# Order of the late gates, the operand pieces and the first ring weights in an output projection

## The chip, the cores and the metric

The kernel runs on one core of a Trainium2 chip. The metric is device time in microseconds (us) of one execution, the median of the runs shown. Five engines work in parallel, each through its own list of instructions in program order, and wait for one another on semaphores: PE (TensorE matmul), DVE (VectorE), ACT (ScalarE), POOL (GpSimd) and SP (SyncE, which here issues DMA loads).

## What is computed

One decoder layer on x of 2 x 512 tokens and 1024 channels: `x = x + block(norm(x))`, then a quantized product with a context, then a feed-forward stage with reconstructed weights. The block, cut to the part that the change touches:

```python
    y = Y.reshape(B, L, D_INNER) * silu(z)
    return y @ w_out.T                       # output projection
...
    h = res + mamba2(h, ...)
    h2 = rmsnorm(h, ln2_w)
    mlp = silu(h2 @ gate_w.T) * (h2 @ up_w.T) @ down_w.T
    return res + mlp
```

## The kernel before

All products are made in a split form: an operand in float32 becomes a rounded "hi" part (made by ACT, a copy to the rounded type) and a "lo" remainder (made by DVE, value minus hi), and three matmuls (hi hi, hi lo, lo hi) stand for one.

**The output projection** is the loop `for n in range(BATCH * KT)` that PE, ACT and DVE each write out for themselves. It has 16 blocks; `h, o = divmod(n, KT)` gives the half of the tokens (h, 0 or 1; the batch element is `ORDER[h]`) and the output tile o (0 to 7). PE does 24 matmuls of 128x512 for a block (8 tiles of the inner dimension times 3, line 857) and counts `s_used` at its end. Weights are double buffered: at the head of turn n, once block n is done, ACT makes the hi part of the weights of block n+2 (`weights_hi`, line 1284) and DVE the lo part (`weights_lo`, line 1738), and PE waits for the latter (`s_ready`) before block n+2. DVE then adds the block's product to the residual (line 2358, `s_h`), ACT squares the sum (`rms_square`, line 1618) and DVE adds up the squares (`rms_add`, line 2336), for a normalization of each half whose sums PE multiplies out with two more matmuls (`rms_sums`, line 1003; for half 0 after block 9, for half 1 later).

**The gates.** What the projection reads is y times silu(z). For half 1 these are made within the blocks of half 0: in turn o, ACT computes silu of tile o (`z_silu`, line 1590) and DVE multiplies (`make_y`, line 2268); one turn later ACT makes the hi part (`y_hi`, line 1586) and DVE the lo part (`y_lo`, line 2273). The eighth tile's hi and lo come at the end of turn 7. Block 8 (half 1, o = 0) needs the tiles in order of k.

**The feed-forward stage** that follows (`plain`, line 1031 for PE) starts on half 0's normalized values. Its operands have names: b11 (channel tiles 0 to 3 of half 0) and b21 (tiles 4 to 7), each of four pieces kk; b12 and b22 are the same of half 1. A piece is made by DVE (`make`, line 1877: residual times a parameter times the root), split by ACT (`part_hi_of`, line 1414) and DVE (`part_lo_of`, line 1906). In the loop of the projection, after the root of half 0 in turn 10 (`rms_root` on ACT, lines 1621 to 1624, `rms_rsqrt` on DVE, lines 2341 to 2344), turn 11 makes all of b11 and turn 13 all of b21. Weights of that stage go through a ring of seven slots: ACT `weight_hi` (line 1361), DVE `weight_lo` through `prefill` (line 1834). The seven slots are filled first in turns 14 and 15 by ACT and at the end of turn 14 by DVE. PE's order after block 15 is two steps of `plain` (12 matmuls each), the two matmuls of `rms_sums(1)`, which wait for the last `rms_add` of half 1, and then the rest of the feed-forward stage.

The order of the work on each engine is thus the order in which these lines are written out; no scheduler moves anything.

Of the kernel before, what the change touches and what calls it, by code (L numbers as in the profile page):

```python
# [8 lines left out]
ALU = mybir.AluOpType  # L9
# [21 lines left out]

ORDER = (1, 0)
Y_AT = {5: (0, 1, 2), 6: (3, 4, 5), 7: (6, 7)}
CTX_TILES = BATCH * KT

PART_AT = (0, 32, 64)
# [151 lines left out]
def build(nc, x_t, ctx, w_mamba, w_dt, w_gu, w_dn, f_gu, f_dn, b_gu, b_dn, params, shapes_only,  # L188
# [127 lines left out]
    def scr_c(j):  # L316
        return scr_c0[:, j, :] if j < 4 else scr_c1[:, j - 4, :]
# [186 lines left out]
    def part_hi(m, name):  # L504
        if name == "b12":
            return THr[m][2]
        return THr[m][3 if name == "b22" and m == 1 else RIGHT.index(name)]
# [4 lines left out]
    def value_of(m, name):  # L512
        if name in ("b11", "t2"):
            return VA[m]
        return TLf[m][{"b21": 6, "t4": 6, "b22": 5, "b12": 4, "t3": 4, "t1": 3}[name]]
# [760 lines left out]
    def _(act):  # L1276
# [125 lines left out]
        def part_hi_of(m, name):  # L1402

            if name == "t2":

                act.wait_ge(s_pd, fw(m, 6, 1) + 1)
            elif name == "t1" and m == 1:
                act.wait_ge(s_pd, fw(m, 7, 1) + 1)
            elif name == "t4":

                act.wait_ge(s_tlo, n_lo(m, "t2", KH - 1))
            for kk in range(KH):
                act.wait_ge(s_tv, N_MAKE[m, name, kk])
                act.activation(part_hi(m, name)[:, kk, :], value_of(m, name)[:, kk, :], ACT.Copy,
                               scale=-1.0 if name == "t2" else 1.0).then_inc(s_thi, 1)

        def move_b22():
            act.wait_ge(s_x2a, 32 * KT)
# [165 lines left out]
        def y_hi(h, k):  # L1584
            act.wait_ge(s_a, h * KT + k + 1)
            act.activation(ah(ORDER[h], k), xbc[:, 4 + k, HALF[ORDER[h]]], ACT.Copy).then_inc(s_ah, 1)

        def z_silu(h, k):
            act.wait_ge(s_z, h * KT + k + 1)
            act.activation(z_tile(h, k), z_tile(h, k), ACT.Silu).then_inc(s_zs, 1)  # L1590
# [29 lines left out]
        def rms_root(h):  # L1620
            act.preload_act_table_set("natural_log_exp_and_others")
            act.wait_ge(s_rv, h + 1)
            own.then(act.activation(rms_t[:, h, :], bank(6 + h), ACT.Ln, bias=EPS, scale=1.0 / DM))
            act.activation(rms_scale[:, h, :], rms_t[:, h, :], ACT.Exp, scale=-0.5).then_inc(s_hroot, 1)

        for n in range(BATCH * KT):
            h, o = divmod(n, KT)
            if N_OUT + n + 2 < N_MLP:
                weights_hi(N_OUT + n + 2, n % 2)
            if h == 0:  # L1630
                z_silu(1, o)
                if o >= 1:
                    y_hi(1, o - 1)
            elif o == 2:
                rms_root(0)
            elif o == 3:
                part_hi_of(0, "b11")
            elif o == 5:
                part_hi_of(0, "b21")
            elif o == 6:  # L1640
                for w in range(4):
                    weight_hi(w)
            elif o == 7:
                for w in range(4, RING):
                    weight_hi(w)
            rms_square(h, o)
            if n == KT - 1:
                y_hi(1, KT - 1)
        rms_root(1)

        feed_forward(0)
# [80 lines left out]
    def _(dve):  # L1732
# [133 lines left out]

        def make(m, name):

            va = VA[m]
            for kk in range(KH):  # L1870
                dst = value_of(m, name)[:, kk, :]
                if name in ("b11", "b12", "b21", "b22"):
                    k = kk if name in ("b11", "b12") else KH + kk
                    col = 0 if name in ("b11", "b21") else 1
                    half = COL[m][col]
                    if m == 0:
                        ins = STT(dst, hres[:, k, half], par[:, PL2 + k:PL2 + k + 1], rms_scale[:, col, :], ALU.mult, ALU.mult)
                    else:
                        ins = TT(dst, xc[:, k, half], scr_c(5)[:, half], ALU.mult)
                elif name == "t1":  # L1880

                    dve.wait_ge(s_tv, N_MAKE[m, "b12", kk])
                    ins = TT(dst, va[:, kk, :], value_of(m, "b12")[:, kk, :], ALU.subtract)
                elif name == "t3":
                    dve.wait_ge(s_tv, N_MAKE[m, "t1", kk])
                    ins = TT(dst, value_of(m, "b22")[:, kk, :], value_of(m, "b12")[:, kk, :], ALU.subtract)
                elif name == "t2":
                    dve.wait_ge(s_tv, N_MAKE[m, "t3", kk])
                    ins = TT(dst, value_of(m, "t3")[:, kk, :], va[:, kk, :], ALU.add)
                else:  # L1890
                    dve.wait_ge(s_tv, N_MAKE[m, "t2", kk])
                    ins = TT(dst, va[:, kk, :], value_of(m, "b21")[:, kk, :], ALU.subtract)
                ins.then_inc(s_tv, 1)
                if name in ("b11", "b21", "b12") and kk >= 1:
                    part_lo_of(m, name, kk - 1)
            if name in ("b11", "b21", "b12"):
                part_lo_of(m, name, KH - 1)

        def part_lo_of(m, name, kk):
            dve.wait_ge(s_thi, n_hi(m, name, kk))  # L1900
            dst, hi = part_lo(m, name)[:, kk, :], part_hi(m, name)[:, kk, :].bitcast(F32)
            src = value_of(m, name)[:, kk, :]
            if name == "t2":
                STT(dst, src, -1.0, hi, ALU.mult, ALU.subtract).then_inc(s_tlo, 1)
            else:
                TT(dst, src, hi, ALU.subtract).then_inc(s_tlo, 1)
# [439 lines left out]
        for n in range(BATCH * KT):  # L2346
            h, o = divmod(n, KT)
            half = HALF[ORDER[h]]
            if N_OUT + n + 2 < N_MLP:
                weights_lo(N_OUT + n + 3, n % 2, n % 2)  # L2350
            if h == 0:
                make_y(1, o)
                if o >= 1:
                    y_lo(1, o - 1)
            if o == 0:
                dve.wait_ge(s_reload[h], 16)
            dve.wait_ge(s_used, N_OUT + n + 1)
            TT(hres[:, o, half], hres[:, o, half], bank(n % 4), ALU.add).then_inc(s_h, 1)
            if o >= 2:
                rms_add(h, o - 1)  # L2360
            if n == KT - 1:
                y_lo(1, KT - 1)
            elif n == KT:
                rms_add(0, KT - 1)
            elif n == KT + 2:
                rms_rsqrt(0)
            elif n == KT + 3:
                make(0, "b11")
            elif n == KT + 5:
                make(0, "b21")  # L2370
            elif n == KT + 6:
                prefill(0, range(RING))
        rms_add(1, KT - 1)
        rms_rsqrt(1)

# [175 lines left out]
```

## Time and profile before

| | |
|---|---|
| median of 3 runs | 2105.76 us (2105.51 to 2106.44) |
| the profiled execution: its own time | 2103.68 us |
| its span in the profile | 2101.5 us |
| PE busy | 2073.0 us, 99% of the span |
| DVE busy | 1678.2 us, 80% |
| ACT busy | 1054.8 us, 50% |
| granted TensorE clock over the span | 0.999 |

The profile gives busy time by engine, a chain of work that ended last, and groups of instructions; the trace behind it answers questions about a stretch: what an engine did in order of time with the idle time in front of each instruction and what ended it (the timeline), who waited for whom (the waits), and busy shares with the granted clock by stretch (the windows). Times in those views count from the start of the span.

### The profile page before, as it was taken

How to read it: one execution, taken by the hardware profiler on the slowest of the kernel's cores; microseconds unless marked ns; L12 is line 12 of the kernel's file. 1: busy time of each engine (PE TensorE's matmuls, PEld its weight loads, DVE VectorE, ACT ScalarE, POOL GpSimd, SP SyncE). 2: the span in 40 equal slices, each digit the busy share in tenths (PEclk: the TensorE clock that was granted, in tenths of full speed). 3: DMA queues.
4: the chain of work that ended last, by engine and by line, in shares of the span. 5: the costliest groups of instructions: out<-in, count | busy, mean ns of one | idle time of the engine just before them, and what ended most of it. 6: DMA issues, size and time to landing. Idle time of an engine off the chain costs nothing.

```text
span 2101.5 us, 26518 instructions
## 1 busy us (share of the span) xinstructions
PE 2073.0 (99%) x9230; PEld 1671.1 (80%) x9234; DVE 1678.2 (80%) x2526; ACT 1054.8 (50%) x1748; POOL 185.3 (9%) x296
## 2 busy tenths in 40 slices
PE   8999999999999999999999999999999999999999
PEld 5777778788888888888888855888888888888887
DVE  7878686797777888888879899977777776698885
ACT  5333244457777777774444366533333333444442
POOL 0001101101111112110000002010000100100000
PEclk9999999999999999999999999999999999999999
DMA  3151116639889999897440045554444443846101
GB/s 136 40 201 60 51 61 200 145 114 324 295 295 335 328 347 350 293 344 264 140 141 1 1 180 127 171 186 147 176 150 174 152 152 126 322 172 211 50 21 61
DMA packets 136434, 370.07 MB, mean 176 GB/s; under 512 B 16688, under 2 KB 27568, under 8 KB 132656
## 3 DMA queue, kind: packets, MB, share of 16 engines
q1 hardware_dynamic: 110640, 287.12, 39.7%
q0 software_dynamic: 25088, 80.23, 11.3%
q8 instruction: 74, 1.21, 0.2%
q10 hardware_dynamic: 576, 1.05, 0.1%
q14 instruction: 56, 0.46, 0.1%
HBM read 288.12 MB, written 84.41 MB: 177 GB/s over the span
## 4 chain that ended last, share of the span: by engine, by line
PE 86%; DVE 9%; ACT 3%; issue 1%; DMA 1%; ACTq 0%; SPq 0%; DVEq 0%
PE pair L1087 47%; PE pair L1135 24%; PE pair L857 7%; PE pair L1031 2%; DVE conv_out L2171 2%; PE pair L850 1%; PE pair L1097 1%; DVE weights_lo L1738 1%; PE pair L969 1%; PE pair L990 1%; DMA sign_in_ab<-sign_spill 1%; PE pair L996 0%; DVE centred L2382 0%; ACT scratch_c L1675 0%; PE pair L992 0%
## 5 line engine op out<-in xcount | busy, mean ns | idle before, releaser
L1087 PE MATMUL pair<-comb_hi,ring_hi 128*128 128x512 f32 x1456 | 566.5, 389 | 0.0
L1087 PE MATMUL pair<-comb_hi,ring_lo 128*128 128x512 f32 x1456 | 566.4, 389 | 0.0
L1087 PE MATMUL pair<-comb_lo,ring_hi 128*128 128x512 f32 x1456 | 566.4, 389 | 0.0
L1135 PE MATMUL pair<-inner_ring_a,ring_hi 128*128 128x512 f32 x1080 | 332.7, 389 | 0.0
L1087 PEld LDWEIGHTS pair<-comb_hi,ring_hi 128*128 128x128 f32 x1456 | 273.3, 188 | 57.2 <-issue 0.4
L1087 PEld LDWEIGHTS pair<-comb_lo,ring_hi 128*128 128x128 f32 x1456 | 273.3, 188 | 57.0
L1087 PEld LDWEIGHTS pair<-comb_hi,ring_lo 128*128 128x128 f32 x1456 | 273.3, 188 | 56.4
L1135 PEld LDWEIGHTS pair<-inner_ring_a,ring_hi 128*128 128x128 f32 x1080 | 202.6, 188 | 41.9
L1135 PE MATMUL pair<-inner_ring_a,ring_lo 128*128 128x512 f32 x540 | 210.1, 389 | 0.0
L1361 ACT ACTIVATE ring_hi<-ring_sum 128x512 fp32r<-128x512 f32 x160 | 100.5, 631 | 148.3 <-DVE ring_sum L1819 146.2
L1834 DVE TENSOR_TENSOR ring_lo<-raw_a,ring_hi 128x512 fp32r<-128x512 f32 x146 | 99.5, 686 | 53.6 <-ACT ring_hi L1361 52.0
L1135 PE MATMUL pair<-inner_ring_b,ring_hi 128*128 128x512 f32 x432 | 133.4, 390 | 0.0
L1135 PEld LDWEIGHTS pair<-inner_ring_a,ring_lo 128*128 128x128 f32 x540 | 101.4, 188 | 21.3
L1834 DVE TENSOR_TENSOR ring_lo<-ring_sum,ring_hi 128x512 fp32r<-128x512 f32 x160 | 109.6, 685 | 9.8 <-ACT ring_hi L1361 8.1
L857 PE MATMUL pair<-act_hi,weights_hi 128*128 128x512 f32 x256 | 108.4, 424 | 1.7 <-DVE act_lo L2273 1.4
L1985 DVE TENSOR_TENSOR pair<-coeff_in 128x1024 f32<-128x1024 f32 x84 | 103.0, 1226 | 0.1
L857 PE MATMUL pair<-act_hi,weights_lo 128*128 128x512 f32 x256 | 99.9, 390 | 0.0
L857 PE MATMUL pair<-act_lo,weights_hi 128*128 128x512 f32 x256 | 99.8, 390 | 0.0
L1487 ACT ACTIVATE sign_out<-pair 128x1024 int8<-128x1024 f32 x84 | 85.3, 1016 | 23.9 <-DVE pair L1985 23.9
L1135 PEld LDWEIGHTS pair<-inner_ring_b,ring_hi 128*128 128x128 f32 x432 | 81.1, 188 | 17.2 <-issue 0.5
L1361 ACT ACTIVATE ring_hi<-raw_a 128x512 fp32r<-128x512 f32 x146 | 87.4, 624 | 10.5 <-DVE raw_a L1814 6.9
L1361 ACT ACTIVATE ring_hi<-comb_hi_f 128x512 fp32r<-128x512 f32 x72 | 45.3, 630 | 93.1 <-PE pair L1135 48.2
(395 smaller groups left out, 3606.4 us busy)
## 6 DMA issues: line engine op xcount, KB each, us to landing
coeff_in<-f_gu SPq DMA_DIRECT2D x56, 512.0 KB, 5.4
coeff_in<-b_gu SPq DMA_DIRECT2D x56, 512.0 KB, 7.2
weights_raw<-w_mamba SPq DMA_DIRECT2D x44, 512.0 KB, 3.5
raw_a<-w_gu SPq DMA_DIRECT2D x28, 512.0 KB, 6.2
raw_a<-w_gu SPq DMA_DIRECT2D x56, 256.0 KB, 6.2
u_spill<-gate_a POOLq DMA_DIRECT2D x56, 256.0 KB, 5.3
coeff_in<-f_dn SPq DMA_DIRECT2D x28, 512.0 KB, 4.7
coeff_in<-b_dn SPq DMA_DIRECT2D x28, 512.0 KB, 7.0
```

Source lines behind the costliest of these rows:

```text
L850: ins = pe.matmul(out[:, HALF[half]], w[:, wi, k * P:(k + 1) * P], a(half, k), start=k == 0 and n == 0, stop=k == KT - 1 and n == 2)
L857: ins = pe.matmul(out, w[:, wi, k * P:(k + 1) * P], a(b, k), start=k == 0 and n == 0, stop=k == KT - 1 and n == 2, skip_group_check=True)
L969: pe.matmul(ps[2][:, g * 512:(g + 1) * 512], bx_cur[:, 2 + g, :], xbc[:, 4 + g * HPG:4 + (g + 1) * HPG, b * SEQ + c * P:b * SEQ + (c + 1) ...
L990: ins = pe.matmul(ps[2][:, hd * P:(hd + 1) * P], x_dt[:, hd, :], att[:, hd, :], start=True, stop=c == 0)
L1031: ins = pe.matmul(out, wt[:, slot, col], a, start=j % 2 == 0 and kk == 0 and n == 0, stop=j % 2 == 1 and kk == KH - 1 and n == 2, skip_gro ...
L1087: ins = pe.matmul(out, wt[:, slot, col], a, start=t in (0, 1, 3) and kk == 0 and n == 0, stop=kk == KH - 1 and n == 2, skip_group_check=True)
L1135: ins = pe.matmul(out, wt[:, slot, col], a, start=t in (0, 1, 3) and k == 0 and n == 0, stop=k == SC_PAIRS - 1 and n == 2, skip_group_chec ...
L1361: act.activation(WRH[:, slot, :], src, ACT.Copy).then_inc(s_whi, 1)
L1487: act.activation(sign_out[:, c % 2, :], dif_ps[:, :], ACT.Sign).then_inc(s_sign, 1)
L1834: TT(WRL[:, slot, :], src, WRH[:, slot, :].bitcast(F32), ALU.subtract).then_inc(s_wlo, 1)
L1985: TT(dif_ps[:, :], dif[:, c % 2, 0, :], dif[:, c % 2, 1, :], ALU.subtract).then_inc(s_cd, 1)
L2171: ins = STT(tile[:, :, back:], src[:, :, :SEQ - back], conv_par[:, s, TAPS - 1 - back:TAPS - back], tile[:, :, back:], ALU.mult, ALU.add)
```

## The change

Nothing is computed differently and no instruction is added or taken away; three things move.

1. The gates of half 1 follow a table, `Y_LATE`: turns 2 and 4 make two tiles, turns 0, 1, 3 and 5 one, and turns 6 and 7 none. The hi and lo parts come one turn after their tile, so the last pair stands in turn 6.
2. b11 and b21 are made in pieces by a table, `PARTS_AT`: one in turn 10 (half 1, o = 2), two each in turns 11, 12 and 13, one in turn 14. The lo part of a piece comes after the next piece is made.
3. The first two of the seven ring weights are split in turn 13 and the other five in turn 14, on ACT and on DVE.

```diff
+Y_LATE = {0: (0,), 1: (1,), 2: (2, 3), 3: (4,), 4: (5, 6), 5: (7,)}
+PARTS_AT = {2: (("b11", 0),), 3: (("b11", 1), ("b11", 2)), 4: (("b11", 3), ("b21", 0)),
+            5: (("b21", 1), ("b21", 2)), 6: (("b21", 3),)}
...
@@ ACT, loop of the projection
             if h == 0:
-                z_silu(1, o)
-                if o >= 1:
-                    y_hi(1, o - 1)
-            elif o == 2:
-                rms_root(0)
-            elif o == 3:
-                part_hi_of(0, "b11")
-            elif o == 5:
-                part_hi_of(0, "b21")
-            elif o == 6:
-                for w in range(4):
-                    weight_hi(w)
-            elif o == 7:
-                for w in range(4, RING):
+                for k in Y_LATE.get(o, ()):
+                    z_silu(1, k)
+                for k in Y_LATE.get(o - 1, ()):
+                    y_hi(1, k)
+            else:
+                if o == 2:
+                    rms_root(0)
+                for name, kk in PARTS_AT.get(o, ()):
+                    part_hi_tile(0, name, kk)
+                for w in {5: range(0, 2), 6: range(2, RING)}.get(o, ()):
                     weight_hi(w)
             rms_square(h, o)
-            if n == KT - 1:
-                y_hi(1, KT - 1)
...
@@ DVE, loop of the projection
             if h == 0:
-                make_y(1, o)
-                if o >= 1:
-                    y_lo(1, o - 1)
+                for k in Y_LATE.get(o, ()):
+                    make_y(1, k)
+                for k in Y_LATE.get(o - 1, ()):
+                    y_lo(1, k)
...
             if o >= 2:
                 rms_add(h, o - 1)
-            if n == KT - 1:
-                y_lo(1, KT - 1)
-            elif n == KT:
+            if n == KT:
                 rms_add(0, KT - 1)
             elif n == KT + 2:
                 rms_rsqrt(0)
-            elif n == KT + 3:
-                make(0, "b11")
-            elif n == KT + 5:
-                make(0, "b21")
-            elif n == KT + 6:
-                prefill(0, range(RING))
+            if h == 1:
+                for name, kk in PARTS_AT.get(o, ()):
+                    make_tile(0, name, kk)
+                    if kk > 0:
+                        part_lo_of(0, name, kk - 1)
+                    elif name == "b21":
+                        part_lo_of(0, "b11", KH - 1)
+                if o == 5:
+                    prefill(0, range(0, 2))
+                elif o == 6:
+                    part_lo_of(0, "b21", KH - 1)
+                    prefill(0, range(2, RING))
```

`part_hi_tile` and `make_tile` are the bodies of the loops over kk in `part_hi_of` and `make`, taken out as functions. The lists of PE, SP and POOL keep their order.

How ACT's list moves, from the hi part of the weights that follows the root of half 0. Before (L1284 is `weights_hi`, L1414 a hi part of an operand piece, L1618 `rms_square`; comb_hi_76 holds b11's hi parts and comb_hi_77 those of b21):

```order
147 L1284 ACTIVATE weights_hi<-weights_raw 128x1024
148 L1414 ACTIVATE comb_hi_76<-comb_hi_f_06_96 128x512 x4
149 L1618 ACTIVATE rms_squares<-h_residual 128x512
150 L1284 ACTIVATE weights_hi<-weights_raw 128x1024
151 L1618 ACTIVATE rms_squares<-h_residual 128x512
152 L1284 ACTIVATE weights_hi<-weights_raw 128x1024
```

Now, from the instruction behind the root (the same lines are L1287, L1420 and L1624):

```order
141 L1630 ACTIVATE rms_scale<-rms_steps 128x512
142 L1420 ACTIVATE comb_hi_76<-comb_hi_f_06_96 128x512
143 L1624 ACTIVATE rms_squares<-h_residual 128x512
144 L1287 ACTIVATE weights_hi<-weights_raw 128x1024
145 L1420 ACTIVATE comb_hi_76<-comb_hi_f_06_96 128x512 x2
146 L1624 ACTIVATE rms_squares<-h_residual 128x512
147 L1287 ACTIVATE weights_hi<-weights_raw 128x1024
148 L1420 ACTIVATE comb_hi_76<-comb_hi_f_06_96 128x512
149 L1420 ACTIVATE comb_hi_77<-comb_lo_f_06_124 128x512
150 L1624 ACTIVATE rms_squares<-h_residual 128x512
151 L1287 ACTIVATE weights_hi<-weights_raw 128x1024
```

Before, one of the three remaining `weights_hi` stood behind operand pieces; now each of the three does.

DVE's list at the end of the loop. Before (L2358 adds a block to the residual, L2336 is `rms_add`, L1834 `weight_lo` of the ring, L1906 the lo part of a piece):

```order
340 L1906 TENSOR_TENSOR comb_lo_105<-comb_lo_f_06_124,comb_hi_77 128x512 x2
341 L2358 TENSOR_TENSOR h_residual<-h_residual,pair 128x512
342 L2336 TENSOR_TENSOR rms_sum<-rms_sum,rms_squares 128x512
343 L1834 TENSOR_TENSOR ring_lo<-raw_a_139,ring_hi 128x512 x4
344 L1834 TENSOR_TENSOR ring_lo<-raw_a_140,ring_hi 128x512 x2
345 L1834 TENSOR_TENSOR ring_lo<-raw_a_141,ring_hi 128x512
346 L2358 TENSOR_TENSOR h_residual<-h_residual,pair 128x512
347 L2336 TENSOR_TENSOR rms_sum<-rms_sum,rms_squares 128x512 x2
```

Now, from the last lo part of turn 13 on (the same lines are L2362, L2339, L1834 and L1909; L1884 makes a piece):

```order
337 L1909 TENSOR_TENSOR comb_lo_105<-comb_lo_f_06_124,comb_hi_77 128x512
338 L1834 TENSOR_TENSOR ring_lo<-raw_a_139,ring_hi 128x512 x2
339 L2362 TENSOR_TENSOR h_residual<-h_residual,pair 128x512
340 L2339 TENSOR_TENSOR rms_sum<-rms_sum,rms_squares 128x512
341 L1884 TENSOR_TENSOR comb_lo_f_06_124<-h_residual,params,rms_scale 128x512
342 L1909 TENSOR_TENSOR comb_lo_105<-comb_lo_f_06_124,comb_hi_77 128x512 x2
343 L1834 TENSOR_TENSOR ring_lo<-raw_a_139,ring_hi 128x512 x2
344 L1834 TENSOR_TENSOR ring_lo<-raw_a_140,ring_hi 128x512 x2
345 L1834 TENSOR_TENSOR ring_lo<-raw_a_141,ring_hi 128x512
346 L2362 TENSOR_TENSOR h_residual<-h_residual,pair 128x512
347 L2339 TENSOR_TENSOR rms_sum<-rms_sum,rms_squares 128x512 x2
```

Two ring weights now stand ahead of the residual add of block 14; the last piece of b21 and its split, and five ring weights, stand between it and the last adds, where before all seven ring weights stood.

## Rows read from the trace of the kernel before

**Rows 1.** The page, busy time of PE
```profile
PE 2073.0 (99%) x9230; PEld 1671.1 (80%) x9234; DVE 1678.2 (80%) x2526; ACT 1054.8 (50%) x1748; POOL 185.3 (9%) x296
```
**Rows 2.** Waits of PE from 320 to 1200 us: total, times, longest
```profile
PE pair L857 <- DVE act_lo L2273: 1.4, 1, 1.4
PE pair L1031 <- issue: 0.7, 1, 0.7
PE pair L857 <- DVE weights_lo L1738: 0.2, 1, 0.2
```
**Rows 3.** PE's timeline: start us, us, instruction, [idle before <- what ended it]
```profile
372.03 0.39 PE L857 MATMUL pair<-act_hi,weights_lo 128*128 128x512 f32 x1
373.83 0.50 PE L857 MATMUL pair<-act_hi,weights_hi 128*128 128x512 f32 x1 [1.42 <-DVE act_lo L2273]
...
402.50 0.39 PE L857 MATMUL pair<-act_hi,weights_lo 128*128 128x512 f32 x1
403.13 0.50 PE L857 MATMUL pair<-act_hi,weights_hi 128*128 128x512 f32 x1 [0.24 <-DVE weights_lo L1738]
...
413.93 0.39 PE L857 MATMUL pair<-act_hi,weights_lo 128*128 128x512 f32 x1
415.01 0.47 PE L1031 MATMUL pair<-comb_hi,ring_hi 128*128 128x512 f32 x1 [0.70 <-issue]
...
420.58 1.12 PE L1003 MATMUL pair<-rms_sum,ones 128*128 128x512 f32 x2
```
**Rows 4.** The chain that ended last, a stretch of two blocks: start, us, what
```profile
381.12 10.91 PE pair L857 x48
```
**Rows 5.** ACT's timeline in turns 10 to 12
```profile
386.67 1.06 ACT L1284 ACTIVATE weights_hi<-weights_raw 128x1024 fp32r<-128x1024 f32 x1 [2.73 <-PE pair L857]
...
392.11 1.06 ACT L1284 ACTIVATE weights_hi<-weights_raw 128x1024 fp32r<-128x1024 f32 x1 [1.28 <-PE pair L857]
...
399.71 0.63 ACT L1414 ACTIVATE comb_hi<-comb_hi_f 128x512 fp32r<-128x512 f32 x1 [0.63 <-DVE comb_hi_f L1877]
400.25 0.61 ACT L1618 ACTIVATE rms_squares<-h_residual 128x512 f32<-128x512 f32 x1
400.77 1.04 ACT L1284 ACTIVATE weights_hi<-weights_raw 128x1024 fp32r<-128x1024 f32 x1
```
**Rows 6.** DVE's timeline in turns 10 to 12
```profile
391.79 0.69 DVE L2344 SCALAR_TENSOR_TENSOR rms_scale<-rms_steps,rms_scale 128x512 f32<-128x512 f32 x1
393.27 1.23 DVE L1738 TENSOR_TENSOR weights_lo<-weights_raw,weights_hi 128x1024 fp32r<-128x1024 f32 x1 [0.79 <-ACT weights_hi L1284]
394.41 0.68 DVE L2358 TENSOR_TENSOR h_residual<-h_residual,pair 128x512 f32<-128x512 f32 x1
395.01 0.69 DVE L2336 TENSOR_TENSOR rms_sum<-rms_sum,rms_squares 128x512 f32<-128x512 f32 x1
...
397.67 0.75 DVE L1877 SCALAR_TENSOR_TENSOR comb_hi_f<-h_residual,params,rms_scale 128x512 f32<-128x512 f32 x1
398.33 0.69 DVE L1906 TENSOR_TENSOR comb_lo<-comb_hi_f,comb_hi 128x512 fp32r<-128x512 f32 x1
```
**Rows 7.** DVE's timeline in turns 14 and 15
```profile
414.23 4.29 DVE L1834 TENSOR_TENSOR ring_lo<-raw_a,ring_hi 128x512 fp32r<-128x512 f32 x7
418.44 0.68 DVE L2358 TENSOR_TENSOR h_residual<-h_residual,pair 128x512 f32<-128x512 f32 x1
419.04 1.48 DVE L2336 TENSOR_TENSOR rms_sum<-rms_sum,rms_squares 128x512 f32<-128x512 f32 x2
```
**Rows 8.** Waits of PE over the whole span: total, times, longest
```profile
PE pair L883 <- DVE act_lo L2096: 3.8, 1, 3.8
...
PE pair L937 <- DVE minus_cs_wide L2232: 2.3, 1, 2.3
```
**Rows 9.** Windows after those two waits: stretch, length, busy, granted clock, DMA share, GB/s
```profile
16.00:19.30 3.30, 3.30 (x8) 2.48 (x9) 3.30 (x6) 2.75 (x5) 0.00 (x0) 0.50 1.04 402
150.60:156.00 5.40, 5.40 (x32) 4.77 (x33) 1.80 (x2) 2.62 (x3) 0.00 (x0) 1.00 0.43 150
```

More of the change, by code:

```diff
@@ L1412, in part_hi_of, with part_hi_tile @@
             for kk in range(KH):
-                act.wait_ge(s_tv, N_MAKE[m, name, kk])
-                act.activation(part_hi(m, name)[:, kk, :], value_of(m, name)[:, kk, :], ACT.Copy,
-                               scale=-1.0 if name == "t2" else 1.0).then_inc(s_thi, 1)
+                part_hi_tile(m, name, kk)
+        def part_hi_tile(m, name, kk):
+            act.wait_ge(s_tv, N_MAKE[m, name, kk])
+            act.activation(part_hi(m, name)[:, kk, :], value_of(m, name)[:, kk, :], ACT.Copy,
+                           scale=-1.0 if name == "t2" else 1.0).then_inc(s_thi, 1)
         def move_b22():
@@ L1867, in make @@
         def make(m, name):
-            va = VA[m]
             for kk in range(KH):
[L1871 to L1893, printed above, removed]
+                make_tile(m, name, kk)
                 if name in ("b11", "b21", "b12") and kk >= 1:
@@ L1897, in make, with make_tile @@
                 part_lo_of(m, name, KH - 1)
+        def make_tile(m, name, kk):
+            va = VA[m]
+            dst = value_of(m, name)[:, kk, :]
+            if name in ("b11", "b12", "b21", "b22"):
+                k = kk if name in ("b11", "b12") else KH + kk
+                col = 0 if name in ("b11", "b21") else 1
+                half = COL[m][col]
+                if m == 0:
+                    ins = STT(dst, hres[:, k, half], par[:, PL2 + k:PL2 + k + 1], rms_scale[:, col, :], ALU.mult, ALU.mult)
+                else:
+                    ins = TT(dst, xc[:, k, half], scr_c(5)[:, half], ALU.mult)
+            elif name == "t1":
+                dve.wait_ge(s_tv, N_MAKE[m, "b12", kk])
+                ins = TT(dst, va[:, kk, :], value_of(m, "b12")[:, kk, :], ALU.subtract)
+            elif name == "t3":
+                dve.wait_ge(s_tv, N_MAKE[m, "t1", kk])
+                ins = TT(dst, value_of(m, "b22")[:, kk, :], value_of(m, "b12")[:, kk, :], ALU.subtract)
+            elif name == "t2":
+                dve.wait_ge(s_tv, N_MAKE[m, "t3", kk])
+                ins = TT(dst, value_of(m, "t3")[:, kk, :], va[:, kk, :], ALU.add)
+            else:
+                dve.wait_ge(s_tv, N_MAKE[m, "t2", kk])
+                ins = TT(dst, va[:, kk, :], value_of(m, "b21")[:, kk, :], ALU.subtract)
+            ins.then_inc(s_tv, 1)
         def part_lo_of(m, name, kk):
```

## The prediction

> **What bounds the kernel now.** The page shows PE busy for 99% of the span [rows 1], so the time can only move by what PE stands still. The waits of PE over the projection and the 800 us behind it are the second view: three waits, all of about a microsecond or less, and nothing else up to 1200 us [rows 2]. So whatever PE loses or gains before about 421 us comes out one for one at the end of the feed-forward stage's first part; nothing behind it is there to swallow it. The third view is PE's timeline at those waits. The unit there is a block: 48 matmuls take 10.91 us [rows 4], so a matmul takes 0.227 us and a block of 24 takes 5.45 us. From start to start, less one matmul, PE loses 1.57 us before block 8's last tile, 0.40 us before block 14, and 0.85 us before the first ring weight [rows 3]. The first matmul after a wait takes 0.50 us where others take 0.39 [rows 3]: 0.11 more each time. Together 1.68 + 0.51 + 0.96 = **3.15 us**, or 0.15% of the time. That is all the change can win. Differences within 0.2%, 4.2 us, are about what a measurement of this kernel cannot tell from no change.
>
> **The change, part by part.** Instructions are the same in kind and number, so nothing is added to any engine's work; only waits can differ.
>
> *The late gates.* The wait removed is the 1.68 us: the eighth tile's lo part is now made in turn 6, a block earlier than the block 8 that reads it. The price is a third gate operation in turns 2 to 5 on ACT and DVE. On DVE a turn then takes 1.14 us for the weights (393.27 to 394.41) and 0.60 each for five further operations (394.41 to 395.01) [rows 6], 4.1 us after ACT's 1.1 us; that is 5.2 of a block's 5.45 us, and weights have a block's length less about 2.3 us to spare. I cost it at nothing; if that cover were gone, the excess of a turn would come on top. So −1.7 us, and all that follows is 1.7 us earlier.
>
> *The pieces of b11 and b21.* Here ACT's order decides: `weights_hi` of the next block stands behind the pieces and the square of this turn, and the pieces wait for DVE, which makes them only after this turn's weights, residual add and square sum. One turn of this ring, in durations of the rows: weights_hi to weights_lo 1.10 us in all with the hand-over (392.11 to 393.27 less DVE's own 0.06) [rows 5, 6]; weights_lo 1.14, residual add 0.60, square sum 0.60, first piece 0.66, lo part of the piece before 0.60 [rows 6]; second piece 0.75 and a hand-over of 0.04 [rows 6]; its hi part on ACT 0.54 and the square 0.52 [rows 5]. The sum is **6.55 us a turn, against PE's block of 5.45**: each turn falls behind by 1.1 us. It starts late as well: in turn 10 the root on DVE ends at 392.5 (less 1.7: 390.8) [rows 6], the first piece needs 0.75, its hi part and the square 1.06, so turn 11's weights_hi starts at 392.6, where it could start at 390.4 (392.11 less 1.7) [rows 5].
> - Block 13's weights (weights_hi 392.6, lo part from 393.7 to 394.9) are in time: PE reaches block 13 at 395.6.
> - Block 14's: weights_hi 399.15, lo part ready at 401.5; PE is there at 401.1 (402.50 + 0.23 − 1.7 [rows 3]). Wait 0.4 us, with the first matmul 0.5. This takes the place of the 0.5 that was there.
> - Block 15's: weights_hi 405.7, lo part ready at 408.1; PE is there at 401.55 + 0.11 + 5.45 = 407.1. Wait 1.0, with the first matmul **1.1 us**, where no wait was.
>
> *The ring weights.* The first two are now ready at 413.1 to 413.6, before block 15 ends at 408.1 + 0.11 + 5.45 = 413.65: the 0.96 us is gone. But what follows on DVE up to the last square sum of half 1 is what `rms_sums(1)` waits for. In turn 13 DVE goes from weights_lo at 406.8: 1.14, residual and square sum 1.20, two pieces and two lo parts 2.53, about 0.7 until ACT has the first ring hi part (it stands behind the second piece's), two ring weights 1.2: 413.6. Then residual and square sum 1.2, last piece 0.66, two lo parts 1.2 with 0.2 of waiting between, five ring weights 3.0 (seven took 4.29 with the last one's tail, 0.60 each), block 15's residual add 0.60, two square sums 1.48 (both from [rows 7]): 421.9. PE comes there after two steps of 12 matmuls, 413.65 + 5.45 = 419.1. **Wait 2.8 us**. Before, PE started these two matmuls at 420.58 [rows 3] and the last sum ended at 420.52 [rows 7]: DVE was already just on time. The block's own adds now come later than before (last sum 421.9 against 420.5), though PE is early.
>
> *The sum.* Removed 3.15; added 0.5 + 1.1 + 2.8 = 4.4; net **+1.3 us**; by the direct comparison, 421.9 against 420.5 for the event that releases PE, +1.4. I take +1.4. The ring of ACT and DVE does not show in the trace in this order, so its bounds are the nearest rows: below, each turn at PE's pace of 5.45 us, with no new wait, −3.15; above, each turn as long as turn 11 of before, where all of b11 stood between two weights_hi (392.11 to 400.77, 8.7 us [rows 5]), which would add 2.1 us in each of the last two turns, +5.6. My 6.55 is a sum of that turn's own operations with two pieces in place of four. Against the profiled execution's 2103.68 us that is 2105.1; against the median, which is 2.1 higher, 2105.76 + 1.4 = **2107.2 us**.
>
> **The rivals.**
> - *The stalls go and no new one comes* (the turns keep PE's pace, and DVE is done with the last sums when PE arrives): −3.15 us, 2102.6. For it: DVE stands idle before its weights in every one of these turns (0.79 us in turn 11 [rows 6]), and ACT is busy for 50% of the span [rows 1]. Against: that idle time is the wait on the ring itself, and the pieces lie on it. It decides by whether a turn takes under 5.45 us. 10%.
> - *Only the block waits come, the one at the sums does not*: if DVE's 14 operations in turns 13 and 14 start earlier than laid out by the 2.8 us, −3.15 + 1.6 = −1.6, 2104.2. For it: a small shift is enough to change who is last, since before the two were within 0.1 us [rows 3, 7]. Against: that stretch is nearly all back to back work on DVE. 12%.
> - *Slower, by the clock*. In this trace a wait of 3.8 us [rows 8] was followed by a stretch of 3.3 us at a granted clock of 0.50 (1.2 GHz), and one of 2.3 us [rows 8] by full clock (2.4 GHz) [rows 9]. The new wait of 2.8 lies between. If the clock falls behind it, 3.3 us of work at half speed cost 1.65 more: +3.1, 2108.9. For it: block 15's wait of 1.0 comes shortly before. Against: the row that 2.8 is nearest to is the one with full clock behind it. What decides is the granted clock behind the sums' matmuls. 10%. 
>
> **How the numbers follow.** The forecast has 65%: 2107.2, by itself 2106.0 to 2108.4 (the layout's hand-overs add up to about 1 us of doubt, and the runs of before spread over 0.9). The range 2104.0 to 2109.2 takes in the second rival and the clock; it leaves out the first (10%), the last (3%) and a few per cent of the others. Under 2101.55 (faster by over 0.2%) only the first rival with a lucky median reaches: 0.03. Over 2109.97 lie the last and a part of the clock's case: 0.05. The rest, 0.92, is the same within 0.2%.
>
> **What would show it.** No wait before block 8; waits of PE on weights_lo before blocks 14 and 15, the second about 1 us; none at the first ring weight; and a new wait of 2 to 3 us of the sums' matmuls on DVE's rms_sum. On ACT, weights_hi of turns 11, 12 and 13 start about 6.55 us apart, with comb_hi waiting some 3.2 us on DVE in each turn. The forecast is wrong if these starts are 5.45 apart, or if the sums' matmuls do not wait; in both cases the kernel is faster than before.

## The result and the profile after

The changed kernel takes 2108.41 us, the median of 22 runs (2106.59 to 2111.05). The kernel before, measured again beside it on the same chip, takes 2105.65 us, also the median of 22 runs (2104.09 to 2107.36). The ratio is 1.0013, with a 95% interval of 1.0008 to 1.0019. The change therefore costs 2.8 us (1.7 to 4.0). The forecast was +1.4, inside the bound of 0.2% but only half of what was measured. Medians in this document leave out single executions that took 2977 us and more, of which e3, e5 and two sets of runs of the kernel before have one each.

The profiled execution of the changed kernel took 2109.04 us, with a span of 2106.9 us. Its page shows PE as full as before [rows 1]:

```profile
PE 2076.5 (99%) x9234; PEld 1672.8 (79%) x9234; DVE 1678.3 (80%) x2526; ACT 1054.7 (50%) x1748; POOL 185.4 (9%) x296
```

PE's waits from 320 to 1200 us (total, times, longest) answer to [rows 2]:

```profile
PE pair L1006 <- DVE rms_sum L2339: 2.7, 1, 2.7
PE pair L860 <- DVE weights_lo L1738: 1.1, 2, 0.8
PE pair L1090 <- ACT gate_a L1445: 0.4, 1, 0.4
```

The waits on act_lo (before block 8) and at the first ring weight are gone. Two waits on weights_lo have come, and a longer one of the sums' matmuls (L1006) on `rms_sum`. The third row is a wait at 692 us, which another execution of the same kernel (g1 below) does not have. PE's timeline at these places answers to [rows 3] (start us, us, instruction, [idle before <- what ended it]):

```profile
401.08 0.39 PE L860 MATMUL pair<-act_hi,weights_lo 128*128 128x512 f32 x1
401.81 0.50 PE L860 MATMUL pair<-act_hi,weights_hi 128*128 128x512 f32 x1 [0.34 <-DVE weights_lo L1738]
...
407.16 0.39 PE L860 MATMUL pair<-act_hi,weights_lo 128*128 128x512 f32 x1
408.34 0.50 PE L860 MATMUL pair<-act_hi,weights_hi 128*128 128x512 f32 x1 [0.79 <-DVE weights_lo L1738]
...
419.15 0.39 PE L1034 MATMUL pair<-comb_hi,ring_lo 128*128 128x512 f32 x1
422.24 2.08 PE L1006 MATMUL pair<-rms_sum,ones 128*128 128x512 f32 x2 [2.71 <-DVE rms_sum L2339]
423.33 1.42 PE L1034 MATMUL pair<-comb_hi,ring_hi 128*128 128x512 f32 x1
424.54 0.63 PE L1034 MATMUL pair<-comb_lo,ring_hi 128*128 128x512 f32 x1
```

From start to start, less one matmul of 0.227 us, PE loses 0.50 us before block 14, 0.95 before block 15 and 2.86 before the sums. The last three rows show something else: the sums' matmuls take 2.08 us, where the same two took 1.12 before [rows 3], and the next one takes 1.42.

To compare executions that begin a few tenths of a microsecond apart, I count from the projection's first matmul (324.13 us here, 323.84 before). On PE's timeline the sums then start at 98.11 us, before at 96.74: +1.37. The first matmul of the product stage (L1090, before L1087) starts at 138.78, before at 135.85: +2.93. So 1.37 us are lost up to the sums and 1.56 us behind them, in 40 us of work that has no wait in it.

PE's windows say what those 1.56 us are (stretch, length, busy time of PE, PEld, DVE, ACT and POOL, granted clock, DMA share, GB/s):

```profile
422.20:425.50 3.30, 3.26 (x6) 1.94 (x7) 0.00 (x0) 1.67 (x3) 0.00 (x0) 0.50 0.62 84
425.60:430.00 4.40, 4.40 (x20) 3.63 (x20) 4.21 (x7) 1.28 (x3) 0.00 (x0) 1.00 0.00 0
```

For 3.3 us behind the wait the granted clock is 0.50 (1.2 GHz), then 1.00 (2.4 GHz) again. Half speed over some 3.3 us costs about 1.65 us, and the places above show 1.56.

The other two engines show why PE waits. ACT's timeline in turns 10 to 13 answers to [rows 5]:

```profile
385.25 1.06 ACT L1287 ACTIVATE weights_hi<-weights_raw 128x1024 fp32r<-128x1024 f32 x1 [2.73 <-PE pair L860]
391.88 0.63 ACT L1420 ACTIVATE comb_hi<-comb_hi_f 128x512 fp32r<-128x512 f32 x1 [3.00 <-DVE comb_hi_f L1884]
392.94 1.04 ACT L1287 ACTIVATE weights_hi<-weights_raw 128x1024 fp32r<-128x1024 f32 x1
397.13 0.63 ACT L1420 ACTIVATE comb_hi<-comb_hi_f 128x512 fp32r<-128x512 f32 x1 [3.15 <-DVE comb_hi_f L1884]
...
399.46 1.04 ACT L1287 ACTIVATE weights_hi<-weights_raw 128x1024 fp32r<-128x1024 f32 x1
403.66 0.63 ACT L1420 ACTIVATE comb_hi<-comb_hi_f 128x512 fp32r<-128x512 f32 x1 [3.15 <-DVE comb_hi_f L1884]
405.98 1.05 ACT L1287 ACTIVATE weights_hi<-weights_raw 128x1024 fp32r<-128x1024 f32 x1
```

In turns 11, 12 and 13 `weights_hi` waits for no PE any more, as it did up to turn 10. It starts behind the pieces, at 392.94, 399.46 and 405.98, 6.52 us apart, and the first `comb_hi` of each turn stands 3.0 to 3.15 us waiting for DVE. PE uses up a block's weights in 5.45 us. DVE's timeline at the end answers to [rows 7]:

```profile
412.63 1.29 DVE L1834 TENSOR_TENSOR ring_lo<-raw_a,ring_hi 128x512 fp32r<-128x512 f32 x2 [0.62 <-ACT ring_hi L1364]
...
417.10 3.09 DVE L1834 TENSOR_TENSOR ring_lo<-raw_a,ring_hi 128x512 fp32r<-128x512 f32 x5
420.11 0.68 DVE L2362 TENSOR_TENSOR h_residual<-h_residual,pair 128x512 f32<-128x512 f32 x1
420.71 1.48 DVE L2339 TENSOR_TENSOR rms_sum<-rms_sum,rms_squares 128x512 f32<-128x512 f32 x2
```

The last sum ends at 422.19, and PE starts the sums' matmuls at 422.24.

### The profile page after: what moved, and what is told of

It is laid out like the page before. It is cut to its first block, busy times and chain, and to the rows that moved or that the text cites. A ratio compares the mean times of both kernels' runs of the same rounds, so it can differ in the third digit from the quotient of the medians.

```text
span 2106.9 us, 26521 instructions
## 1 busy us (share of the span) xinstructions
PE 2076.5 (99%) x9234; PEld 1672.8 (79%) x9234; DVE 1678.3 (80%) x2526; ACT 1054.7 (50%) x1748; POOL 185.4 (9%) x296
## 4 chain that ended last, share of the span: by engine, by line
PE 84%; DVE 10%; ACT 3%; issue 1%; DMA 1%; ACTq 0%; SPq 0%; DVEq 0%
PE pair L1090 46%; PE pair L1138 24%; PE pair L860 7%; PE pair L1034 2%; DVE conv_out L2174 2%; PE pair L853 1%; PE pair L1100 1%; PE pair L972 1%; DVE weights_lo L1738 1%; PE pair L993 1%; DMA sign_in_ab<-sign_spill 1%; DVE ring_lo L1834 1%; PE pair L999 0%; DVE centred L2390 0%; DMA ctx_in<-ctx 0%
## 5 line engine op out<-in xcount | busy, mean ns | idle before, releaser
L1090 PE MATMUL pair<-comb_hi,ring_hi 128*128 128x512 f32 x1456 | 567.0, 389 | 0.4 <-ACT gate_a L1445 0.4
L1090 PE MATMUL pair<-comb_hi,ring_lo 128*128 128x512 f32 x1456 | 566.9, 389 | 0.0
L1090 PE MATMUL pair<-comb_lo,ring_hi 128*128 128x512 f32 x1456 | 566.8, 389 | 0.0
L1090 PEld LDWEIGHTS pair<-comb_hi,ring_hi 128*128 128x128 f32 x1456 | 273.4, 188 | 58.2 <-DVE ring_lo L1834 0.8
L1090 PEld LDWEIGHTS pair<-comb_hi,ring_lo 128*128 128x128 f32 x1456 | 273.4, 188 | 56.8
L1090 PEld LDWEIGHTS pair<-comb_lo,ring_hi 128*128 128x128 f32 x1456 | 273.4, 188 | 56.5
L1834 DVE TENSOR_TENSOR ring_lo<-raw_a,ring_hi 128x512 fp32r<-128x512 f32 x146 | 99.6, 686 | 54.6 <-ACT ring_hi L1364 52.9
L1834 DVE TENSOR_TENSOR ring_lo<-ring_sum,ring_hi 128x512 fp32r<-128x512 f32 x160 | 109.6, 685 | 9.8 <-ACT ring_hi L1364 7.8
```

The lines of the kernel that those rows point to most:

```text
L1090: ins = pe.matmul(out, wt[:, slot, col], a, start=t in (0, 1, 3) and kk == 0 and n == 0, stop=kk == KH - 1 and n == 2, skip_group_check=True)
L1834: TT(WRL[:, slot, :], src, WRH[:, slot, :].bitcast(F32), ALU.subtract).then_inc(s_wlo, 1)
```

## The experiments

Two theories stood against each other at first. The first: each of the three parts does what was laid out, the gates win 1.7 us, and the pieces lose it and more through the ring of ACT and DVE and through DVE's queue ahead of the last sum. The rival: the time beyond +1.4 is a cost of something else, the clock behind the new wait being the candidate. All kernels below were timed beside the kernel before. "Sums" and "product" are the starts of those two matmuls after the projection's first one, in the profiled execution.

**e1_gates_only: the late gates alone**, in the kernel before.

```diff
+Y_LATE = {0: (0,), 1: (1,), 2: (2, 3), 3: (4,), 4: (5, 6), 5: (7,)}
...
-                z_silu(1, o)
-                if o >= 1:
-                    y_hi(1, o - 1)
+                for k in Y_LATE.get(o, ()):
+                    z_silu(1, k)
+                for k in Y_LATE.get(o - 1, ()):
+                    y_hi(1, k)
...
-                make_y(1, o)
-                if o >= 1:
-                    y_lo(1, o - 1)
+                for k in Y_LATE.get(o, ()):
+                    make_y(1, k)
+                for k in Y_LATE.get(o - 1, ()):
+                    y_lo(1, k)
...
```

The hi and lo parts of the eighth tile at the end of turn 7 fall away with it.

> The kernel before with the late gates alone moved (two to a block); the operand pieces and the ring weights stay as before. Layout theory: the wait before block 8's last tile goes and nothing else changes, so PE reaches every later point 1.7 us earlier: time before minus 1.7 us (about 2104.0), the waits before block 14 (0.5) and the first ring weight (0.9) still there. Rival (the late gates overfill the turns of the first half, or the gained time is given back at the next wait): no wait before block 8, but a longer one before block 14 or at the sums, and the time of before within 0.5 us.

Measured: 2103.80 us against 2105.45, ratio 0.9993 (0.9985 to 1.0002). Sums at 95.07, product at 134.20: 1.67 and 1.65 us earlier than before. PE's waits from 320 to 470 us:

```profile
PE pair L1032 <- issue: 0.7, 1, 0.7
PE pair L858 <- DVE weights_lo L1738: 0.2, 1, 0.2
```

Block 8's wait is gone and the other two stand as they were. The gain of 1.7 us is all kept at the product stage, though the medians alone do not separate it from nothing.

**e2_sums_first: five ring weights moved in the changed kernel**, four of them behind the last square sum on DVE, and on ACT behind the table load of the root.

```diff
-        def rms_root(h):
+        def rms_root(h, ws=()):
             act.preload_act_table_set("natural_log_exp_and_others")
+            for w in ws:
+                weight_hi(w)
...
-                for w in {5: range(0, 2), 6: range(2, RING)}.get(o, ()):
+                for w in {5: range(0, 2), 6: range(2, 3)}.get(o, ()):
...
-        rms_root(1)
+        rms_root(1, range(3, RING))
...
-                    prefill(0, range(2, RING))
+                    prefill(0, range(2, 3))
         rms_add(1, KT - 1)
+        prefill(0, range(3, RING))
```

> The changed kernel with the last five ring weights reordered: one of them ahead of block 15's residual add and the last square sums, four behind them (on ACT behind the table load of the second root). Layout theory: the wait of PE at the sums falls from 2.9 to about 0.5 us, so 2.4 us are gained; the block waits of 0.5 and 0.95 stay. Clock theory (the half clock of 3.4 us after that wait is its consequence): the half clock goes too, another 1.4 to 1.7 us, in all about 4 us under the changed kernel, near 2104.4. Rival (the half clock has nothing to do with this wait): 2.4 us under the changed kernel, 2106.0, with the half clock still at 422 us.

Measured: 2106.26 us against 2105.45, ratio 1.0002 (0.9993 to 1.0011). The wait of the sums fell to 0.3 us and the sums start at 95.71, 1.03 us earlier than before. But the product starts at 136.28, 0.43 later than before: 1.46 us were given back between them, at full clock. The chain of waits of this kernel from 420 us shows where (start us, us, what):

```profile
420.64 1.28 ACT L1627
421.93 2.19 ACT ring_hi L1364 x4
...
427.48 0.76 DVE comb_lo_f L1886
...
433.52 2.07 DVE comb_lo_f L1886 x3
435.59 0.61 DVE ring_lo L1836
436.21 0.04 issue
436.25 23.84 PE pair L1034 x99
```

The four hi parts now stand ahead of half 1's root on ACT, so the operands that DVE makes from that root are late, and PE pays at 436.25 and four times more by 459.13, in each case with a first matmul of 0.50 us. The wait at the sums could be moved, but what was moved behind it went onto the path to the next operands.

**e3_piece_ahead: pieces made a turn before they are split.** In the changed kernel DVE now makes two pieces in each of turns 10 to 13, and their hi and lo parts are taken one turn later.

```diff
-PARTS_AT = {2: (("b11", 0),), 3: (("b11", 1), ("b11", 2)), 4: (("b11", 3), ("b21", 0)),
-            5: (("b21", 1), ("b21", 2)), 6: (("b21", 3),)}
+PARTS_AT = {2: (("b11", 0), ("b11", 1)), 3: (("b11", 2), ("b11", 3)), 4: (("b21", 0), ("b21", 1)),
+            5: (("b21", 2), ("b21", 3))}
...
-                for name, kk in PARTS_AT.get(o, ()):
+                for name, kk in PARTS_AT.get(o - 1, ()):
                     part_hi_tile(0, name, kk)
...
+                for name, kk in PARTS_AT.get(o - 1, ()):
+                    part_lo_of(0, name, kk)
                 for name, kk in PARTS_AT.get(o, ()):
                     make_tile(0, name, kk)
-                    if kk > 0:
-                        part_lo_of(0, name, kk - 1)
...
```

> The changed kernel with each pair of operand pieces made by DVE one turn before ACT and DVE split it, so that ACT finds it ready and the next block's weights never stand behind a wait. Layout theory: turns 11 to 13 keep PE's pace (weights_hi 5.45 us apart instead of 6.5), none of the waits before blocks 8, 14, 15, at the first ring weight and at the sums is left; 3.15 us under the kernel before, about 2102.5. Rival (DVE's queue itself is too full in turns 11 to 14, and not the hand-over from DVE to ACT in front of weights_hi): block waits or the wait at the sums stay within 0.5 us of what they are in the changed kernel.

Measured: 2102.65 us against 2105.45, ratio 0.9985 (0.9976 to 0.9994). Sums at 93.52, product at 132.58: 3.22 and 3.27 us earlier than before. ACT's timeline in turns 11 to 13 of this kernel:

```profile
391.80 1.06 ACT L1287 ACTIVATE weights_hi<-weights_raw 128x1024 fp32r<-128x1024 f32 x1 [1.28 <-PE pair L860]
392.99 1.30 ACT L1420 ACTIVATE comb_hi<-comb_hi_f 128x512 fp32r<-128x512 f32 x2
...
397.24 1.06 ACT L1287 ACTIVATE weights_hi<-weights_raw 128x1024 fp32r<-128x1024 f32 x1 [1.22 <-PE pair L860]
...
402.68 1.06 ACT L1287 ACTIVATE weights_hi<-weights_raw 128x1024 fp32r<-128x1024 f32 x1 [1.79 <-PE pair L860]
```

`comb_hi` finds its piece ready, `weights_hi` waits for PE again and starts 5.44 us apart. PE has no wait at all from 320 to 470 us, and the sums follow without one:

```profile
418.75 1.02 PE L1006 MATMUL pair<-rms_sum,ones 128*128 128x512 f32 x2
```

So it was the wait of ACT on a fresh piece, with `weights_hi` behind it, that made the ring, and not the number of operations: DVE makes and splits two pieces in each of turns 11 to 13 in both kernels. The wait at the sums went with it: DVE's last sum ends at 417.35, 1.4 us ahead of PE. A part of that is that turn 14 has one piece less to make here (0.66 us, made in turn 10 instead). The whole 3.15 us that lay there before were to be had.

**h3_ahead_again** is the same kernel, run again.

> The kernel with each pair of operand pieces made one turn before it is split, once more, for a narrower interval: no wait of PE from the projection's first matmul to the first product, which comes 132.6 us after it (135.85 before), and about 2.8 us under the kernel before.

Measured: 2102.38 us against 2105.20, ratio 0.9986 (0.9976 to 0.9995); sums at 93.54, product at 132.60. This version beats both kernels.

**e5_four_adds: a wait at the sums in the kernel before.** Four adds whose result nobody reads stand on DVE ahead of the last square sum; **g2_five_adds** has five of them.

```diff
+        for _ in range(4):
+            own.then(TT(rms_t[:, 0, :], rms_scale[:, 0, :], rms_scale[:, 0, :], ALU.add))
         rms_add(1, KT - 1)
```

> The kernel before with four adds of 128x512 on DVE, each awaiting the one before (0.73 us), ahead of the very last square sum; they write scratch that nobody reads. PE then waits about 2.8 us at the sums, as in the changed kernel, and nothing else differs from before. Wait alone: 2.7 us over the kernel before. Clock theory: the granted clock falls to 0.5 for 3.4 us right behind that wait, as in the changed kernel, and 1.4 to 1.7 us come on top: 4.1 to 4.4 us over the kernel before, about 2110.

Measured: 2107.74 us against 2105.45, ratio 1.0013 (1.0004 to 1.0022). Sums at 99.49 (+2.75), product at 138.60 (+2.75). A wait of PE of 2.73 us, counted as above, and full clock behind it: 39.11 us from the sums to the product, as before.

**g1_again: the changed kernel once more**, and g2 beside it.

> The changed kernel once more, for a second profile and more runs. If the half clock behind the wait at the sums belongs to this program and not to one execution, it is there again (granted clock 0.5 for 3.4 us from about 422 us), and the time is again some 2.7 us over the kernel before: 1.4 us of waits and 1.3 of clock. If it was chance, the clock stays full at that place; the waits are the same in either case (0.51, 0.95 and 2.87 us).

Measured: 2108.36 us against 2105.46, ratio 1.0016 (1.0007 to 1.0025). Sums at 98.14, product at 138.87: the wait of 2.88 us and the 3.4 us of half clock behind it are there again.

> The kernel before with five adds (0.73 us each, one after the other) ahead of the last square sum in place of four: a wait of 3.46 us at the sums instead of 2.73. Wait alone: 0.73 us over the run with four adds, 3.4 us over the kernel before. Clock theory, by which a longer wait at this place brings the half clock behind it more often: half clock at the sums, 5.1 us over the kernel before.

Measured: 2108.69 us against 2105.46, ratio 1.0021 (1.0012 to 1.003). Sums at 100.27, product at 139.40. The wait is 3.44 us, longer than that of the changed kernel, and the window behind it has full clock:

```profile
424.70:428.10 3.40, 3.32 (x13) 2.43 (x14) 0.86 (x3) 1.23 (x2) 0.00 (x0) 1.00 0.03 5
```

So a wait as long as this does not lower the clock by its length alone.

**g3_two_behind: only two ring weights behind the last square sum on DVE**, the rest as in the changed kernel.

```diff
-                    prefill(0, range(2, RING))
+                    prefill(0, range(2, 5))
         rms_add(1, KT - 1)
+        prefill(0, range(5, RING))
```

> The changed kernel with the lo parts of the last two ring weights, on DVE alone, behind the last square sums; DVE stands idle there anyway, waiting for the root. Layout theory: block 15's residual add comes 1.2 us earlier, and the last square sum then waits for ACT's squares, so the wait at the sums falls from 2.87 to about 1.6, with no new wait behind it: 1.2 us under the changed kernel by waits. Clock theory: no half clock behind a wait of 1.6, another 1.2 us on average: about 2106.0. Rival: the half clock stays at its place, 2107.2.

Measured: 2105.44 us against 2105.46, ratio 1.0002 (0.9993 to 1.0011). Sums at 97.03, product at 136.14: the wait is 1.78 us, 1.1 us less, and there is no half clock. Two ring weights of 0.60 us less in DVE's queue ahead of the sums give back 1.1 us there, and another 1.5 by the clock.

**g4_gates_ring: the gates and the split of the ring weights**, without the pieces. To e1 it adds on ACT and DVE:

```diff
-            elif o == 6:
-                for w in range(4):
+                for w in range(2):
                     weight_hi(w)
-            elif o == 7:
-                for w in range(4, RING):
+            elif o == 6:
+                for w in range(2, RING):
                     weight_hi(w)
...
                 make(0, "b21")
+                prefill(0, range(2))
             elif n == KT + 6:
-                prefill(0, range(RING))
+                prefill(0, range(2, RING))
```

> The kernel before with the late gates moved and the ring weights split two and five as in the change, but the operand pieces made as before (all of b11 in turn 11, all of b21 in turn 13). Layout theory: the wait before the first ring weight (0.88 us) goes, but DVE reaches the last square sum no sooner, since it has the same work ahead of it, so a wait of about 1.0 us appears at the sums in its place; PE passes the sums at the same time as with the late gates alone, 1.7 us under the kernel before. Rival (the two ring weights are a gain of their own): no wait at the sums and 2.6 us under the kernel before.

Measured: 2103.87 us against 2105.46, ratio 0.9994 (0.9985 to 1.0003). Sums at 95.03, product at 134.14, the same as e1 within 0.06 us. The wait at the first ring weight is gone, and this one has come in its place:

```profile
PE pair L1004 <- DVE rms_sum L2335: 0.8, 1, 0.8
```

The split alone wins nothing: what it hands to PE earlier, PE spends waiting for a DVE queue that ends when it did. The pieces then are the difference between g4 and the changed kernel: 98.11 less 95.03, or 3.08 us at the sums.

**h1_no_gates: the changed kernel with the gates one to a block again**, the reverse of e1's edit.

> The changed kernel with the late gates put back to one a block (part 1 of the change undone, parts 2 and 3 kept). Layout theory: the wait of 1.58 us before block 8 returns, and the waits before blocks 14 and 15 and at the sums stay at 0.5, 0.95 and 2.9 us, 1.7 us later each; PE starts the sums 99.8 us after the projection's first matmul (98.1 in the changed kernel). If the half clock belongs to a wait of this length behind these block waits, it comes again: 1.7 us over the changed kernel, 2110.1. If it hangs on where in time the wait falls, it can be gone: the first product 138.8 us after the projection's first matmul, as in the changed kernel, and the time of the changed kernel or under it.

Measured: 2108.86 us against 2105.20, ratio 1.0018 (1.0009 to 1.0027). Sums at 99.85, product at 139.00. Block 8's wait of 1.4 us is back, the waits on weights_lo (1.1 us in two) and at the sums (2.7) are those of the changed kernel, and the sums come 1.74 us later than there. At the product only 0.22 us of that are left, because this kernel has full clock behind its wait, which is as long (2.88 us) and comes behind the same two block waits:

```profile
424.80:428.20 3.40, 3.34 (x13) 2.46 (x14) 0.85 (x3) 1.80 (x3) 0.00 (x0) 1.00 0.61 82
```

**h2_one_add: the changed kernel with one unread add ahead of the last square sum**, in the manner of e5.

> The changed kernel with one more add of 128x512 on DVE (0.73 us, awaited, its result unread) ahead of the last square sum: the wait at the sums grows from 2.87 to about 3.4 us, at the same place in time. Waits alone: 0.5 us over the changed kernel. The half clock should be there in the profile, as in both profiles of the changed kernel; if it is gone, it was chance there.

Measured: 2109.46 us against 2105.20, ratio 1.0021 (1.0012 to 1.003). Sums at 98.62, product at 139.10: a wait of 3.41 us, and half clock from 422.15 us on. Here the clock fell while PE still waited, as its window shows (columns as above, busy PE first, granted clock third from the end); the sums start at 422.61:

```profile
422.15:422.60 0.45, 0.00 (x0) 0.00 (x0) 0.41 (x1) 0.44 (x1) 0.00 (x0) 0.50 1.17 73
```

In g1 it fell 0.4 us after the sums had begun at 423.00:

```profile
423.00:423.40 0.40, 0.40 (x1) 0.30 (x2) 0.00 (x0) 0.40 (x1) 0.00 (x0) 1.00 1.12 72
423.45:423.90 0.45, 0.45 (x3) 0.26 (x1) 0.00 (x0) 0.07 (x1) 0.00 (x0) 0.50 0.57 73
```

Of the 4.3 us that h2's median lies over the kernel before, 3.25 are there at the product; where the rest lies was not found out.

The clock's part side by side, from the profiled executions (wait counted from start to start less a matmul):

| kernel | wait at the sums, us | sums start after the projection's start, us | sums to product, us | granted clock for 3.3 us |
|---|---|---|---|---|
| g3 | 1.78 | 97.03 | 39.11 | 1.00 |
| after | 2.87 | 98.11 | 40.67 | 0.50 |
| g1 (same kernel) | 2.88 | 98.14 | 40.73 | 0.50 |
| h2 | 3.41 | 98.62 | 40.47 | 0.50 |
| e5 | 2.73 | 99.49 | 39.11 | 1.00 |
| h1 | 2.88 | 99.85 | 39.14 | 1.00 |
| g2 | 3.44 | 100.27 | 39.13 | 1.00 |

The three that fell are not those with the longest waits (g2's is the longest), nor those with block waits shortly ahead (h1 has them too). They are those whose wait ends 98.1 to 98.6 us after the start, and the fall itself comes 98.0 us (after), 98.1 (h2) and 98.6 (g1) after it, whether PE still waits then or not. Among the waits of 2.7 us and more, what separates the two groups in this table is the moment; whether it is the cause, and by what rule, stays open. The executions without a profile point the same way: each has its mean granted clock on record, to three places. Over the runs of the changed kernel, g1 and h2 these average 0.9974 to 0.9976, over those of every other kernel here 0.9979 to 0.9985, and 3.4 us at half clock in 2106 us would be 0.0008.

## Why the prediction was right, and where its size fell short

- **The late gates, −1.7 us: right.** e1 shows 1.67 us at the sums, h1 1.74 by the reverse edit. The third gate in a turn cost nothing that shows at the sums.
- **The ring of the pieces, 6.55 us a turn: right.** The starts of `weights_hi`, forecast at 392.6, 399.15 and 405.7, came at 392.94, 399.46 and 405.98, with this execution's projection starting 0.29 us later than before. Block 14's wait was 0.50 and block 15's 0.95, forecast 0.4 and 1.0. Each came with a first matmul 0.11 longer. e3 shows the cause: with the pieces made a turn ahead, the turns are 5.44 us apart and both waits are gone.
- **The ring weights and the wait at the sums: right.** The 0.96 us at the first ring weight went (its first matmul took 0.47 us and not 0.50 [rows 3], so the prediction's own reckoning gives 0.93), and 2.86 us came at the sums, forecast 2.8. The last sum was laid out at 421.9 and ended at 422.19. g4 shows that the split by itself only moves PE's wait from one place to the other. That DVE's queue ahead of the last sum sets the wait is shown by g3 (less in it, 1.1 us less) and h2 (one add more, 0.5 us more).
- **The net at the sums: right.** Removed 3.15, added 0.61 + 1.06 + 2.86 = 4.53, net 1.38 by these rows; the sums' start shows 1.37, the forecast was 1.3 to 1.4.
- **The clock: the term that was missed.** The forecast took full clock behind the new wait, because 2.8 us is nearer to the row of 2.3 us with full clock than to that of 3.8 us with half [rows 8, 9]. The rival with half clock got 10%, with +1.65 us on top, +3.1 in all. In three profiles of three with the sums at this moment the clock fell, and by the first product matmul the kernel was 2.93 us later, 1.56 of it behind the wait. So the rival came on top of the forecast, and its size was right. The measured 2108.41 is at the upper end of the forecast's own 2106.0 to 2108.4, and well inside the range only because that was drawn to take in this rival. The failed step is the choice by the nearest wait's length: e5, h1 and g2 show waits of 2.73 to 3.44 us with full clock behind them, so length does not order the cases. The prediction's first sentence falls with it, that the time can only move by what PE stands still: from 422.20 to 425.50 PE is busy for 3.26 of 3.30 us, at half speed. The changed kernel agrees with the first (1.56 us behind a wait of 2.87), these three were paid once, and that the moment separates them fits the second, which no run here tests by itself.
- **The other rivals fell.** That the stalls go and no new one comes (−3.15) is not what this change does, but it is what e3 does. That only the block waits come is refuted by the wait of 2.86 us at the sums.
- **What would have shown it wrong** (turns of `weights_hi` 5.45 us apart, sums that do not wait) are seen, among the kernels with the pieces, only in e3 and its repeat h3, and these are faster, as the text said.

The profiled executions differ by more than the medians, 2109.04 less 2103.68, or 5.4 us. 0.3 of that lies ahead of the projection and 2.93 from there to the product stage. Of the 2.1 us that are left, 1.6 is a stretch near 1289 us at half clock that this execution has and the other has not (the last section shows it), and 0.4 is the wait at 692 us. Over the runs the whole difference is 2.8 us, as the 2.93 at the product stage has it.

## What to carry to other kernels

When a list of one engine puts an operation that waits for fresh work of another engine ahead of one that a third engine needs each turn, lay out one full turn of that ring and compare it with the third engine's pace: 6.55 against 5.45 us here, though ACT was half idle. Making the fresh work one turn earlier than it is used breaks the ring without changing one operation. With the gates and the ring weights moved in the same way, it brought the sums 1.5 us earlier than the pieces as they were made before (93.52 in e3, 95.03 in g4), and the same pieces without that lead brought them 3.08 us later (98.11); all three parts with the lead won 2.8 us of time. A wait that is removed wins only what the next event in the queue allows (g4), and a new wait on a full TensorE should be priced with a half-clock stretch behind it as a case of real weight, not a remote one.

## What was not expected of the hardware

The granted clock behind a wait did not follow the wait's length. A wait of 2.87 us was followed by half clock in each profile of the changed kernel, and a wait of 3.44 us, 2.2 us later after the projection's start, by full clock (the table above). The same shows further on, at a wait that the change does not touch: the statistics' matmuls wait 2.02 us on `x_mid` in both kernels. The kernel before, PE's timeline and the window behind:

```profile
1284.01 2.81 PE L1162 MATMUL pair<-x_mid,ones_over_dm 128*128 128x512 f32 x6 [2.03 <-DVE x_mid L2399]
```

```profile
1284.00:1287.50 3.50, 3.49 (x8) 1.61 (x9) 3.40 (x6) 1.23 (x2) 0.00 (x0) 1.00 0.24 91
```

The kernel after:

```profile
1288.08 4.42 PE L1165 MATMUL pair<-x_mid,ones_over_dm 128*128 128x512 f32 x6 [2.02 <-DVE x_mid L2407]
```

```profile
1289.00:1292.50 3.50, 3.50 (x6) 1.41 (x5) 3.40 (x7) 1.86 (x3) 0.00 (x0) 0.52 0.00 0
```

Six matmuls take 2.81 us in the one and 4.42 in the other, behind the same wait. Nor is it the kernel: g1, the same kernel as after, waits 2.02 us there and has six matmuls in 2.81 us at full clock. So the same wait of 2 us can be followed by half clock in one execution and not in another, and two executions can differ by over a microsecond at such a place with no change in what is computed there. What decides it was not found out.
